# First stage of a graph layer: x statistics moved ahead of the bias rows, weight loads moved ahead of a vector load, transposes over four PSUM banks

## The reference, cut to what matters

```
xn = _layernorm(x, axis=-1)                     # x is 1250 x 512, float32
x = x + gnn(xn, src, dst, W_self, W_neigh, b) + mix(xn, W_qkv, b_qkv, W_out, b_out)
x = x + ffn(_layernorm(x, axis=-1), ...)        # routed experts, cross attention, MLP

gnn:  relu(xn @ W_self.T + (segment_sum(xn[src], dst) / deg) @ W_neigh.T + b)
mix:  q, k, v = split(xn @ W_qkv.T + b_qkv); k = softmax(k over nodes)
      out = (q @ (k.T @ v)) @ W_out.T + b_out
```

## Time and profile before

| | us |
|---|---|
| median of 3 runs | 2025.42 |
| the runs | 2022.64, 2025.42, 4704.47 |
| profiled execution, its own time | 2021.58 |
| its span on the core | 2019.8 |
| PE busy | 1863.3 (92%) |
| DVE busy | 1180.1 (58%) |

### The profile page before, as it was taken

One profiled execution on the slowest core, in us unless ns is written; L12 is line 12 of the kernel. 1 busy time (PEld: TensorE's weight loads), 2 busy tenths in 40 slices (PEclk: granted clock), 3 DMA queues, 4 the chain that ended last, 5 costly groups with the idle time before them and its releaser, 6 DMA issues.

```text
span 2019.8 us, 31328 instructions
## 1 busy us (share of the span) xinstructions
PE 1863.3 (92%) x10595; PEld 1655.1 (82%) x10595; DVE 1180.1 (58%) x2333; ACT 729.2 (36%) x1381; POOL 356.7 (18%) x345
## 2 busy tenths in 40 slices
PE   1899989975999999999999999989999999999998
PEld 0678657863899999989899898879999989788996
DVE  6577568784556554573746647546565556566332
ACT  0223211023564445445454544245454544221110
POOL 3210001024122102020100003200000004356340
PEclk9999989987899999999999999989999999999999
DMA  3101001012021100020000000100000000202111
GB/s 105 32 7 42 11 6 36 1 47 93 11 113 27 32 27 6 1 88 37 12 11 11 12 1 3 35 11 6 11 6 12 6 1 27 88 31 68 43 32 51
DMA packets 25045, 60.58 MB, mean 30 GB/s; under 512 B 2548, under 2 KB 4816, under 8 KB 24149
## 3 DMA queue, kind: packets, MB, share of 16 engines
q1 hardware_dynamic: 24910, 58.74, 8.8%
HBM read 44.87 MB, written 13.86 MB: 29 GB/s over the span
## 4 chain that ended last, share of the span: by engine, by line
PE 81%; DVE 9%; issue 2%; POOL 2%; ACT 2%; DVEq 1%; DMA 1%; SPq 1%; POOLq 0%; ACTq 0%
PE ps L2283 20%; PE ps L2168 13%; PE ps L2338 7%; PE ps L2265 5%; PE ps L2269 5%; PE ps L1972 5%; PE ps L2226 5%; PE ps L2367 4%; PE ps L2086 3%; PE ps L2052 3%; DVE max_part L1728 3%; PE ps L2247 2%; DVE share L1745 2%; PE ps L1985 2%; PE ps L2294 1%
## 5 line engine op out<-in xcount | busy, mean ns | idle before, releaser
L2283 PE MATMUL ps<-p_raw,v_ones 125*128 125x250 f32 x2080 | 535.6, 379 | 4.3 <-DVE feat L1747 2.4
L1728 DVE TENSOR_REDUCE max_part<-ps 125x2 f32<-125x500 f32 x520 | 330.0, 674 | 285.4 <-PE ps L2226 270.0
L1304 ACT ACTIVATE p_raw<-ps 125x500 f32<-125x500 f32 x520 | 304.7, 586 | 357.4 <-PE ps L2269 353.8
L2283 PEld LDWEIGHTS ps<-p_raw,v_ones 125*128 125x128 f32 x2080 | 362.6, 191 | 34.3 <-issue 3.2
L1745 DVE RECIPROCAL share<-ps 64x250 f32<-64x250 f32 x120 | 206.7, 1722 | 64.7 <-PE ps L2283 61.9
L2265 PE MATMUL ps<-q_both_a,k_both_a 128*125 128x250 f32 x520 | 184.2, 374 | 1.8 <-ACT q_row_b L1277 1.8
L2265 PE MATMUL ps<-q_both_b,k_both_b 128*125 128x250 f32 x520 | 181.4, 370 | 0.0
L902 POOL CAST w_hi<-w_raw 128x512 fp32r<-128x512 f32 x44 | 28.2, 640 | 817.0 <-PE ps L2269 358.0
L1569 DVE TENSOR_SCALAR onehot<-iota_h,win_key,key_t 125x320 f16 x453 | 169.1, 373 | 0.7 <-issue 0.6
L2168 PE MATMUL ps<-xa_hi,w_hi 128*128 128x418 f32 (+1 forms) x448 | 152.0, 339 | 18.3 <-POOL w_lo L904 13.9
L1568 DVE TENSOR_SCALAR onehot<-iota_h,low_t 125x125 f16 x453 | 127.6, 282 | 58.4 <-PE ps L2086 29.7
(11 more groups left out here) (375 smaller groups left out, 3476.1 us busy)
## 6 DMA issues: line engine op xcount, KB each, us to landing
w_raw<-in_w_mlp SPq DMA_DIRECT2D x32, 256.0 KB, 2.6
w_raw<-in_w_gps SPq DMA_DIRECT2D x16, 256.0 KB, 2.6
w_raw<-in_w_tp SPq DMA_DIRECT2D x16, 256.0 KB, 2.6
w_raw<-in_w_sp SPq DMA_DIRECT2D x12, 256.0 KB, 2.9
w_raw<-in_w_cr SPq DMA_DIRECT2D x12, 256.0 KB, 2.6
d_xt<-xb_hi SPq DMA_DIRECT2D x1, 2508.0 KB, 7.4
d_xt<-xb_lo SPq DMA_DIRECT2D x1, 2508.0 KB, 14.9
xa_hi<-d_xt SPq DMA_DIRECT2D x1, 2508.0 KB, 9.9
```

Of the source, the lines that this page charges most:

```text
L1304: act.activation(p_raw[:, g % PR, :], ps[0:TOK, g % 2, 0:4 * TOK], ACT.Exp, scale=SCALE).then_inc(s_exp, 1)
L1728: dve.tensor_reduce(part[:, y, :, j], ps[0:TOK, bank, 0:4 * TOK].rearrange("p (h k) -> p h k", h=2), AX.X, ALU.max)\
L2283: ins = pe.matmul(ps[:, bank, 0:2 * TOK], v_ones[:, kt, h, :], p_raw[:, g % PR, cols], start=(b == 0 and x == 0), stop=last)
```

## The change

- SP: the first three weight blocks go out directly behind x; `vecs` and the six rows follow.
- ACT: a square root of one column of `small` is placed at the very start, where ACT waits for nothing but DVE's first constants.
- DVE: the bias rows move from before the statistics of x to behind the last `xa_lo`.
- PE, ACT and DVE: the groups of transposes go round four banks (6, 7, 0, 1) instead of two, and PE waits before group m for DVE's group m - 4.

```diff
--- before.py
+++ after.py
@@ -710,6 +710,7 @@
 
         TR2 = 12
         TR_BANK = (6, 7, 4, 1)
+        X_BANK = (6, 7, 0, 1)
         FIRST_ROWS = NT - 1
         XB_AT = {3 + 3 * x: x for x in range(2 * FB)}
 
@@ -749,7 +750,6 @@
             x_dram = A["x"].rearrange("(t p) d -> p t d", p=TOK)
             for b, (t0, nt) in enumerate(TB):
                 sp.dma_start(tok_a[:, t0:t0 + nt, :], x_dram[:, t0:t0 + nt, :]).then_inc(s_ld_x[b], 16)
-            sp.dma_start(vecs[:, :], A["vecs"]).then_inc(s_ld_vec, 16)
 
             def weights(k, source, slot=None):
 
@@ -761,10 +761,13 @@
             def block_of(name, index):
                 return A[name][bass.ds(index, 1), :, :].rearrange("o p n -> (o p) n")
 
+            for k in range(3):
+                weights(k, block_of("w_gps", k))
+            sp.dma_start(vecs[:, :], A["vecs"]).then_inc(s_ld_vec, 16)
             sp.wait_ge(s_zero, 1)
             for p, x, y in ((0, 0, 0), (32, 0, 0), (64, 0, 1), (96, 0, 1), (0, 1, 2), (32, 1, 2)):
                 sp.dma_start(raw_rows[p:p + 1, x, :], A["rows_gps"][y:y + 1, :]).then_inc(s_ld_row, 16)
-            for k in range(16):
+            for k in range(3, 16):
                 weights(k, block_of("w_gps", k))
             sp.wait_ge(s_side, SIDE_NO["kt", FB - 1, 2])
             sp.dma_start(q_rows[:, :, :], A["w_gps"][16:20, :, :].rearrange("c p n -> p c n")).then_inc(s_ld_q, 16)
@@ -1098,7 +1101,8 @@
                 for t0, nt in TB:
                     for f in range(FB):
                         act.wait_ge(s_tr, m + 1)
-                        act.activation(xa_hi[:, f, t0 * TOK:(t0 + nt) * TOK], ps[:, 6 + m % 2, 0:nt * TOK], ACT.Copy).then_inc(s_tr_act, 1)
+                        act.activation(xa_hi[:, f, t0 * TOK:(t0 + nt) * TOK], ps[:, X_BANK[m % 4], 0:nt * TOK], ACT.Copy)\
+                            .then_inc(s_tr_act, 1)
                         m += 1
 
             def set_in(m):
@@ -1113,6 +1117,7 @@
                     act.wait_ge(s_tok, 2)
                 act.activation(z_feat[:, f, span], src, ACT.Copy).then_inc(s_tr_act, 1)
 
+            act.activation(small[:, 0:1], small[:, 5:6], ACT.Sqrt)
             ln_root(0)
             features_in()
 
@@ -1465,7 +1470,7 @@
                     for f in range(FB):
                         span = slice(t0 * TOK, (t0 + nt) * TOK)
                         dve.wait_ge(s_tr_act, m + 1)
-                        dve.tensor_tensor(xa_lo[:, f, span], ps[:, 6 + m % 2, 0:nt * TOK], f32(xa_hi[:, f, span]), ALU.subtract)\
+                        dve.tensor_tensor(xa_lo[:, f, span], ps[:, X_BANK[m % 4], 0:nt * TOK], f32(xa_hi[:, f, span]), ALU.subtract)\
                             .then_inc(s_tr_dve, 1)
                         m += 1
 
@@ -1534,14 +1539,6 @@
             dve.wait_ge(s_edge, done[0])
             assert done[0] == EDGE_DONE
             dve.tensor_copy(small[:, 7:8], small[:, 5:6]).then_inc(s_hot_free, RING)
-            dve.wait_ge(s_ld_row, 96)
-            dve.tensor_copy(row_mix[:, :], raw_rows[:, 0, :]).then_inc(s_row, 1)
-            dve.tensor_copy(row_gnn[:, :], raw_rows[:, 1, :]).then_inc(s_row, 1)
-            dve.memset(raw_ones[:, :], 1.0).then_inc(s_row, 1)
-            dve.wait_ge(s_row, 3)
-            for p, row, x in ((32, row_mix, 0), (96, row_mix, 0), (32, row_gnn, 1)):
-                dve.tensor_tensor(row[p:p + 1, :], raw_rows[p:p + 1, x, :], f32(row[p:p + 1, :]), ALU.subtract).then_inc(s_row, 1)
-            dve.tensor_copy(ones_r[:, :], raw_ones[:, :]).then_inc(s_row, 1)
             for t in range(NT):
                 if t in (0, 4, 8):
                     dve.wait_ge(s_ld_x[t // 4], 16)
@@ -1552,6 +1549,14 @@
             for t in range(NT):
                 normed(tok_a, tok_a, t, 0)
             features_lo()
+            dve.wait_ge(s_ld_row, 96)
+            dve.tensor_copy(row_mix[:, :], raw_rows[:, 0, :]).then_inc(s_row, 1)
+            dve.tensor_copy(row_gnn[:, :], raw_rows[:, 1, :]).then_inc(s_row, 1)
+            dve.memset(raw_ones[:, :], 1.0).then_inc(s_row, 1)
+            dve.wait_ge(s_row, 3)
+            for p, row, x in ((32, row_mix, 0), (96, row_mix, 0), (32, row_gnn, 1)):
+                dve.tensor_tensor(row[p:p + 1, :], raw_rows[p:p + 1, x, :], f32(row[p:p + 1, :]), ALU.subtract).then_inc(s_row, 1)
+            dve.tensor_copy(ones_r[:, :], raw_ones[:, :]).then_inc(s_row, 1)
             dve.memset(near_rows[:, :, :, D // 2:D // 2 + 1], 1.0).then_inc(s_one_col, 1)
 
 
@@ -1930,10 +1935,10 @@
                 for t0, nt in TB:
                     pe.wait_ge(s_ln_done, t0 + nt)
                     for f in range(FB):
-                        if m >= 2:
-                            pe.wait_ge(s_tr_dve, m - 1)
+                        if m >= 4:
+                            pe.wait_ge(s_tr_dve, m - 3)
                         for t in range(nt):
-                            ins = pe.transpose(ps[:, 6 + m % 2, t * TOK:(t + 1) * TOK],
+                            ins = pe.transpose(ps[:, X_BANK[m % 4], t * TOK:(t + 1) * TOK],
                                                tok_a[:, t0 + t, 128 * f:128 * f + 128], ident[0:TOK, 0:TOK])
                         ins.then_inc(s_tr, 1)
                         m += 1
```

## The result

| | before | changed |
|---|---|---|
| median of 5 runs, us | 2023.42 | 2010.28 |
| the runs, us | 2021.74 to 2025.42, one of 4704.47 | 2009.20 to 2012.44 |
| span of the profiled execution, us | 2019.8 | 2007.4 |
| ratio, 95% interval | | 0.9936 [0.9925, 0.9948] |

The changed kernel is 0.6% faster: the interval excludes no change, and the gain is well under 2%. It takes 2010.28 us where 2010.2 was forecast.

What follows compares the result with a forecast made beforehand. PE was busy 92% with only the first slice low, so the bound was how early its dense work begins. 11.7 + 1.3 + 5.3 - 5.0 = 13.3 us off 2023.5 gave 2010.2, range 2000 to 2020.

Steps and rivals of the forecast that it cites:

- Part 1: DVE's statistics of x run as x lands, ahead of the bias rows, ending at 27.8 instead of 39.46: gain 11.7 us.
- late bound: Latest landing of x, 27.4, when the rows behind it released DVE; the statistics then gain 10.8 us.
- Part 2: ACT's table load of 1.28 us moves to the start, where ACT has no work: gain 1.3 us.
- Part 3: Turn of x over four banks, last normalisation to last subtraction: 6.8 us instead of 12.15, gain 5.3 (3.8 to 6.1).
- Part 4: The earlier layer norm on DVE collides with POOL's weight splits: loss 5.0 us, bounds 2.7 and 8.6.
- The rate of 0.65 per operation: DVE's time per operation beside POOL's splits, from eleven one-hot operations in 7.1 us; seventeen operations would take 11.1 us.
- no collision: Rival: POOL gives way to DVE in the layer norm, 18.3 us gained, 2005.2 us; chance 0.13.
- full blocking: Rival: the layer norm's collision with POOL costs 8.6 us, 9.7 gained, 2013.8 us; chance 0.17.
- an earlier clock: Rival: the denser turn brings PE's higher clock from the first key matmul, 2.5 us more, 2007.7 us; chance 0.05.
- slower than before: Rival: PE's gaps meet clock drops differently, each further stretch costing 3.4 us; with five, 2027 us; chance 0.04.

Runs made afterwards that it cites:

- POOL waiting: The changed kernel in which POOL splits the first key block, then waits for the last normalisation before the next splits: 2002.81 us.
- two-bank kernel: The changed kernel with the transposes going round banks 6 and 7 alone, with the old wait: 2016.93 us.
- the gaps filled: The two-bank kernel with idle PE products: 64 before the turn, 48 behind the first pair of groups, 8 behind each later pair: 2012.50 us.

## Why the prediction was right in total, and where its terms were off

| step | forecast gain | measured | from |
|---|---|---|---|
| 1, statistics end earlier | 11.7 | 10.9 | 39.46 - 28.58 |
| 2, table | 1.3 | 1.34 | 1.63 - 0.29 |
| 3, turn | 5.3 | 5.15 | 12.15 - 7.0 |
| 4, collision | -5.0 | -6.4 | small operations -2.7, normalisations -3.65 |
| first key matmul | 13.3 | 10.97 | 60.31 - 49.34 |
| faster first keys | 0 | 2.54 | 13.51 - 10.97 |
| third key copy | 13.3 | 13.51 | 69.97 - 56.46 |

**Part 1** was right in mechanism: x now sets the end of the statistics. I had taken x and `vecs` as landing together, at 26.5; the last block came at 27.29, near the late bound. The experiment with `vecs` first gives 26.66, so the estimate was good for the old queue order. What was wrong is the sentence that the weight blocks cannot delay x because they stand behind it in its own queue: the last block lands 0.4 to 0.9 us later in the seven profiles with the weights ahead than in the one without. Standing behind in a queue is not the same as moving after.

**Part 2** was right at DVE's wait, 1.34 against 1.3. The experiment without the early root adds what the sum left out: behind that wait lies the collision, which gave nine tenths of a microsecond back.

**Part 3** was right in size, 7.0 against 6.8, but the path in the sum was not quite the one that ran. I had let PE's 5.2 us for groups 4 to 11 set the time. In the trace DVE waits only three times in the turn, 0.47 us in all, and works the rest, and with POOL waiting it doesn't wait at all: its twelve subtractions fill 6.12 us, which was the forecast's lower bound (6.0). PE was also faster than the forecast took it to be, through the clock, which I had not counted there; how much of the turn's gain that gave with four banks isn't measured apart. The sign of it: the fastest transpose of the turn takes 270 ns, where before none took under 415, nor in the two-bank kernel. The answer of the trace for the transposes of the changed kernel (durations in ns, least, middle and most):

```profile
L1941 PE MATMUL ps<-ident,tok_a x40: 270/415/442, 38.4 to 48.1; 125*128 125x125 f32 x40
```

And for the two-bank kernel:

```profile
L1941 PE MATMUL ps<-ident,tok_a x40: 415/415/470, 38.7 to 53.4; 125*128 125x125 f32 x40
```

**Part 4** is the term that was mis-sized: 6.4 us instead of 5.0, inside its bounds. The rate of 0.65 per operation was partly a miscount: between 127.35 and 134.44 the kernel before starts ten one-hot operations, not eleven (the eleventh is the one that begins at 134.44), so they took 0.71 each. Seventeen at 0.71 less the undisturbed 6.1 is 6.0. (The last nine of them, beside three whole splits, took 0.66 each, so the rate also depends on where one cuts.) In the layer norm the seven small operations took 0.6 each (together 4.2 us) and the normalisations 0.83, of which they need 0.46 on their own.

POOL loses little. Its twelve instructions took 12.05 us beside the layer norm. They took 12.75 in the kernel before, but there the first ones ran beside the bias rows, with casts of 1.07; the last three splits of that kernel, beside the statistics, took 5.74 us, so six take about 11.5 undisturbed. POOL lost about 0.6 us and DVE 6.4. In the changed kernel a cast beside a normalisation takes 0.80 and not 0.61:

```profile
35.74 0.80 POOL L905 CAST set_hi<-w_raw 128x512 fp32r<-128x512 f32 x1
```

The experiment with POOL waiting shows the term at its size, and the sizes of the rivals, no collision (0) and full blocking (8.6), both fell.

**The rival "an earlier clock"**, with 0.05, came true beside the forecast, not in place of it, and at its price: 2.5 us. It deserved more. The profile spoke for it: before the change the level was low behind a turn in which PE waited at every pair, and the change took just these waits out. The mistake was to weigh it as a case of its own when it follows from part 3. The experiment with the gaps filled shows the cause.

So the first key matmul was forecast at 47.0 and came at 49.34, and the keys gave 2.5 back: errors of -0.8, -1.4 and -0.15 against +2.5. By the test that I had set, the prediction is wrong where the first key matmul moves by one amount and the end of the span by another. It did: 10.97 and 12.4. The total is right by cancelling.

**Bias rows.** They run from 49.11 to 52.42, 3.3 us instead of 6.1, since POOL is idle by then, and are over long before the third key copy at 56.46. PE never waits for them. That edit cost nothing, as forecast.

**The rest of the span** doesn't pass the shift on unchanged. Two stretches between the same instructions, before (length, busy time and count by PE, PEld, DVE, ACT and POOL, PEclk, DMA share, GB/s):

```profile
97.60:1101.84 1004.24, 943.35 (x5357) 818.46 (x5358) 616.83 (x1492) 383.42 (x746) 137.69 (x131) 0.96 0.09 31
1101.84:1791.61 689.77, 655.63 (x4027) 607.81 (x4026) 408.10 (x602) 307.28 (x593) 97.82 (x107) 0.98 0.05 16
```

And in the changed kernel:

```profile
83.11:1085.40 1002.29, 939.39 (x5357) 815.38 (x5358) 616.14 (x1492) 383.05 (x745) 137.53 (x131) 0.97 0.09 31
1085.40:1779.13 693.73, 659.56 (x4027) 611.10 (x4025) 408.10 (x602) 307.00 (x592) 97.62 (x107) 0.97 0.05 16
```

The shift is 14.5 us at the first of these instructions, 16.4 at the second and 12.5 at the third. PE does the same 5357 and 4027 matmuls with 4.0 us less and then 3.9 us more busy time, and the granted clock moves with it. The 14.5 has its own such piece: where the kernel before has 6.9 us at half clock, this one has 0.76 over 7 us, which is 3.4 us at half clock.

```profile
64.00:71.00 7.00, 4.17 (x11) 3.01 (x12) 7.00 (x19) 0.00 (x0) 4.28 (x5) 0.76 0.46 127
```

A second profile of the changed kernel repeats the pattern (939.68 and 659.77 us of PE in the same two stretches, 0.78 over the 7 us), and its third instruction comes only 0.8 us later, so the drops belong to the kernel and not to one execution. That is the mechanism of the rival "slower than before", of the size forecast for one stretch (steps of 2 to 4 us), but with both signs; the 12.4 at the end is within about 1 us of the 13.5 at the keys. Why the drops lie where they lie is open: no experiment moved them on purpose.

## What to carry to other kernels

Moving work into an idle stretch of one engine is only half a sum: look up which other engine works there, and price the collision per instruction on both engines (here nearly all on DVE, 0.46 to 0.83 us per normalisation). Where a wait falls on a load, compare its GB/s and DMA share with the best stretch of the same trace before rearranging the work around it: cutting 125 partitions into 112 and 13 gained 12 us, nearly as much as the whole change. And when an edit makes PE dense, count the clock of what follows as part of that edit.

## What the runs showed of the hardware that was not expected

- Three loads of 125 partitions moved 126 GB/s with a DMA share of 0.32; six loads of 112 and 13 moved 267 GB/s with 1.06. SP also took 8.56 us to issue the three and 2.74 to issue the six.
- Transposes alone raised PE's level: in the dense turn of the changed kernel the fastest takes 270 ns, and no filler ran there. The Trainium skill (TensorE: Matmul & The Clock Gate, Part 4: PE-mode transpose) says that the full level doesn't engage for the transpose mode; this trace, of float32 transposes, disagrees, and the measurement decides.
- The higher level was gone after PE had stood 3.50 us (eight transposes 1.07 before, 1.93 after). PEclk showed this fall (0.50 from 41 us). But ahead of the first change that a profile records it can mislead: it reads 1.00 in the turns of the kernel before and of the two-bank kernel, where transposes take 415 ns and keys stand 0.35 apart. There only spacing and durations tell.
- Beside POOL's splits, DVE operations of 125x20 elements, 0.18 us alone, took up to 1.25, while statistics (0.60 each) and subtractions from PSUM (6.12 for twelve) kept their pace, and POOL lost about 0.6 us over six splits.
